# Cutting 1160 weight columns into groups of 136, 512 and 512 instead of 392, 384 and 384

## What is computed

```python
# first layer
W = L0_cond_weights[itok_B_0_15]                     # 64x64 for each of the 128 sequences
c = einsum('bct,bcd->bdt', x, W)                     # condition product
logits = c @ W_router.T                              # 8 experts
combine = normalized top-2 of softmax(logits)
h = einsum('nd,erd->ner', c, A)                      # adapters down: 8 experts x rank 16
expert_out = einsum('ner,eor->no', h * combine, B) * 2.0   # adapters up
x = x + c @ W_base.T + b_base + expert_out
# second layer
r = x @ base_weight.T + base_bias + (x @ A1[id].T) @ B1[id].T
x = x + (fp8(r / s_in) @ fp8(weight / s_w)) * (s_in * s_w) + bias
```

## Time and profile before

| | us |
|---|---|
| median of 3 runs | 1992.07 |
| lowest and highest | 1991.67, 1996.24 |
| the profiled execution | 1999.07 |
| its span, first to last instruction | 1997.3 |
| TensorE busy in it | 1970.6 |
| VectorE busy | 1424.8 |
| GpSimd busy | 494.8 |
| ScalarE busy | 399.9 |
| granted TensorE clock, mean | 0.997 |

### The profile page before, as it was taken

One profiled execution on the slowest core, in us unless ns is written; L12 is line 12 of the kernel. 1 busy time (PEld: TensorE's weight loads), 2 busy tenths in 40 slices (PEclk: granted clock), 3 DMA queues, 4 the chain that ended last, 5 costly groups with the idle time before them and its releaser, 6 DMA issues.

```text
span 1997.3 us, 37836 instructions
## 1 busy us (share of the span) xinstructions
PE 1970.6 (99%) x13056; PEld 1808.4 (91%) x13056; DVE 1424.8 (71%) x3877; ACT 399.9 (20%) x1087; POOL 494.8 (25%) x471
## 2 busy tenths in 40 slices
PE   6999999999999999999999999999999999999998
PEld 6999999999999999999988888888888888888886
DVE  7766666777777877766666677767776677667776
ACT  3111111121211112111121221222122212122121
POOL 2553444111011011011122222222222222222221
PEclk9999999999999999999999999999999999999999
DMA  6764444333433433433366556655665565655663
GB/s 210 224 208 151 125 121 133 113 105 117 127 105 105 136 108 105 123 108 97 110 178 161 155 164 166 158 160 155 171 160 163 150 170 163 157 159 160 168 159 104
DMA packets 220535, 290.16 MB, mean 145 GB/s; under 512 B 98103, under 2 KB 169785, under 8 KB 220477
## 3 DMA queue, kind: packets, MB, share of 16 engines
q1 hardware_dynamic: 220476, 289.57, 50.9%
HBM read 163.63 MB, written 109.06 MB: 137 GB/s over the span
## 4 chain that ended last, share of the span: by engine, by line
PE 95%; DVE 2%; SPq 1%; issue 1%; DMA 1%; POOL 0%; ACT 0%; DVEq 0%; ACTq 0%; POOLq 0%
PE bank_g L1027 13%; PE bank_g L1029 13%; PE bank_g L1028 13%; PE bank_g L1091 12%; PE bank_g L1090 12%; PE bank_g L1089 12%; PE bank_y L1102 11%; PE bank_y L1007 3%; PE bank_g L1135 1%; PE bank_g L1059 1%; PE bank_g L1057 1%; PE bank_g L1058 1%; DVE hwt L327 0%; DVE w0l L769 0%; PE bank_y L1111 0%
## 5 line engine op out<-in xcount | busy, mean ns | idle before, releaser
L1027 PE MATMUL bank_g<-w0h,st_h 128*128 128x384 f32 (+1 forms) x1536 | 524.7, 342 | 8.8 <-DMA wpair<-wc 3.8
L1029 PE MATMUL bank_g<-w0h,st_l 128*128 128x384 f32 (+1 forms) x1536 | 520.6, 339 | 0.0
L1028 PE MATMUL bank_g<-w0l,st_h 128*128 128x384 f32 (+1 forms) x1536 | 520.4, 339 | 0.0
L1089 PE MATMUL bank_g<-w1h,st_h 128*128 128x352 f32 x1536 | 505.2, 329 | 0.4 <-ACT val L717 0.4
L1091 PE MATMUL bank_g<-w1h,st_l 128*128 128x352 f32 x1536 | 496.0, 323 | 0.0
L1090 PE MATMUL bank_g<-w1l,st_h 128*128 128x352 f32 x1536 | 495.1, 322 | 0.0
L1027 PEld LDWEIGHTS bank_g<-w0h,st_h 128*128 128x128 f32 x1536 | 288.9, 188 | 24.1 <-issue 15.9
L775 DVE TENSOR_TENSOR st_l<-ring,st_h 128x512 fp32r<-128x512 f32 x128 | 143.1, 1118 | 227.8 <-ACT st_h L700 227.7
L1089 PEld LDWEIGHTS bank_g<-w1h,st_h 128*128 128x128 f32 x1536 | 288.6, 188 | 8.0 <-issue 0.7
L563 POOL TENSOR_TENSOR ring<-ring,b_base_sb 128x1024 f32<-128x1024 f32 x64 | 152.6, 2399 | 563.8 <-PE bank_y L1007 535.0
L1090 PEld LDWEIGHTS bank_g<-w1l,st_h 128*128 128x128 f32 x1536 | 288.3, 188 | 1.6
(11 more groups left out here) (78 smaller groups left out, 1974.4 us busy)
## 6 DMA issues: line engine op xcount, KB each, us to landing
ring<-x SPq DMA_DIRECT2D x64, 512.0 KB, 4.4
x_scratch<-ring SPq DMA_DIRECT2D x64, 512.0 KB, 2.7
x1t_scratch<-x_blocks SPq DMA_DIRECT2D x256, 128.0 KB, 2.5
ring<-x1t_scratch SPq DMA_DIRECT2D x64, 512.0 KB, 3.6
ring<-x_scratch SPq DMA_DIRECT2D x64, 512.0 KB, 5.1
out<-obuf SPq DMA_DIRECT2D x64, 512.0 KB, 2.7
b_stack<-b_split SPq DMA_DIRECT2D x384, 64.0 KB, 3.5
raw<-a_split SPq DMA_DIRECT2D x128, 128.0 KB, 4.2
```

The source lines that it names most:

```text
L1027: pe.matmul(to, st_h[:, rows], w0h[:, k, cols], start=(k == 0), stop=False)
L1028: pe.matmul(to, st_h[:, rows], w0l[:, k, cols], start=False, stop=False)
L1029: last = pe.matmul(to, st_l[:, rows], w0h[:, k, cols], start=False, stop=(k == KC - 1))
L1089: pe.matmul(to, st_h[:, rows], w1h_k[:, k, cols], start=(k == 0), stop=False)
```

## The change

The 136 adapter and router columns become group 0 alone, and the 1024 output columns are cut into two groups of 512. Nothing is left in bank 0 that goes to the output. So:

- The adapters' up products go into banks 1 and 2 only, three matmuls of 512 columns for each.
- VectorE adds two banks of 512 columns to the tile instead of three (256, 384, 384). The remainder st_l of the next tile's second half stands behind the addition of group 1, which is now the first.
- TensorE's group 0 waits for hw_done of the previous tile, where it waited for x1_done[0]; so does the first tile of the second layer.
- The weight pieces of the first tile are 8 of 136 columns and 16 of 512.

```diff
-G0_START = (0, 392, 776)
-G0_WIDTH = (392, 384, 384)
-G0_OUT = (ER + EXPERTS, 0, 0)
-G0_COL = (0, 256, 640)
+G0_START = (0, ER + EXPERTS, ER + EXPERTS + HALF)
+G0_WIDTH = (ER + EXPERTS, HALF, HALF)
+OUT_GROUPS = (1, 2)
...
                     dve.wait_ge(xb_done, n)
-                    for g in range(3):
+                    for g in OUT_GROUPS:
                         dve.wait_ge(acc_ps[g], n)
-                        width = G0_WIDTH[g] - G0_OUT[g]
-                        cols = slice(G0_COL[g], G0_COL[g] + width)
-                        dve.tensor_tensor(ring[:, r, cols], bank_g[:, g, G0_OUT[g]:G0_WIDTH[g]],
+                        cols = slice((g - 1) * HALF, g * HALF)
+                        dve.tensor_tensor(ring[:, r, cols], bank_g[:, g, :],
                                           ring[:, r, cols], ALU.add).then_inc(x1_done[g], 1)
-                        if g == 0 and more:
+                        if g == 1 and more:
                             st_lo(n, 1)
-                        elif g == 0:
+                        elif g == 1:
                             turned_lo(0, 0, 1)
...
                     for g in range(3):
-                        if prior:
+                        if prior and g == 0:
+
+                            pe.wait_ge(hw_done, t)
+                        elif prior:
 
                             pe.wait_ge(x1_done[g], t)
                         last = bank(g, n, prior, pair if g == 1 else ())
...
-                    for g in range(3):
-                        to = bank_g[:, g, G0_OUT[g]:G0_WIDTH[g]]
-                        cols = slice(G0_COL[g], G0_COL[g] + G0_WIDTH[g] - G0_OUT[g])
+                    for g in OUT_GROUPS:
+                        to = bank_g[:, g, :]
+                        cols = slice((g - 1) * HALF, g * HALF)
...
                     if lag:
                         pe.wait_ge(val_done[g], t)
+                    elif g == 0:
+                        pe.wait_ge(hw_done, TILES)
                     else:
                         pe.wait_ge(x1_done[g], TILES)
```

## The result

| | before | changed |
|---|---|---|
| median, us | 1993.55 | 2065.32 |
| lowest and highest | 1991.67, 1996.24 | 2064.6, 2066.11 |
| ratio, 95% interval | | 1.0357 [1.0341, 1.0372] |
| profiled execution, its span | 1999.07, 1997.3 | 2066.11, 2064.3 |

The changed kernel is 71.8 us slower. The forecast was 2051, with a range of 2030 to 2073.

What follows compares the result with a forecast made beforehand. TensorE's start-to-start spacings bound the kernel: wide products +2.52 and narrow -1.53 us a tile make +0.99, x 64 = +63 us, less 4.5 of waits, so 1992 + 59 = 2051.0 us, range 2030 to 2073.

Steps and rivals of the forecast that it cites:

- What bounds the kernel: First layer: TensorE, busy 300.00 of 300.00 us at full clock; a tile is the sum of start-to-start spacings, 14.14 us.
- Narrow products: Group 0, 24 products of 136 columns a tile: 115 ns each, 2.76 us against 4.29, -1.53 us a tile.
- Wide products: 54 products of 512 columns a tile: 229 ns each, 12.37 us against 9.85, +2.52 us a tile.
- The sum: Narrow and wide products together: 15.13 us a tile against 14.14, +0.99, x 64 = +63 us (+43 to +79).
- Waits that go: TensorE's waits for turned router weights in the second tile and for the bank 0 addition at two tiles: -4.5 us together.
- The first tile: The 3.8 us wait for a condition matrix stays, hanging on SyncE's queue; 2 us left either way.
- The remainder: VectorE's rounding remainder for the next tile's second half: ready at T + 2.3, wanted at T + 2.75, so no cost.
- a difference of spacings carries over: The +59 us holds against the median of 1992.07 as against the profiled execution's 1999.07, 0.35% above it.
- Columns alone: Rival: the load costs nothing beyond the stream, a narrow product takes 71 ns; about 1987 to 1989 us. Chance 0.06.
- A quicker load: Rival: a load occupies only 89 ns, which a narrow product then takes; about 2011 us. Chance 0.03.
- load and product in a row: Rival: the load is not hidden, a narrow product takes 188 or 245 ns; 2163 or 2250 us. Chance 0.11.

Runs made afterwards that it cites:

- the long row: 24 32-bit products of one width, appended behind the changed kernel's last matmul with nothing else running: 117.1 ns each at 256 columns, 230.9 at 512.
- the sweep: Changed kernel with rows of 24 matmuls appended, 512 down to 32 columns, plus shorter stationary operands and bf16: 32-bit spacings from 230.9 ns at 512 to 111.2 at 136.
- The run of bf16: Changed kernel with group 0's matmuls reading the upper halves of both 32-bit operands as bf16, same widths: 2029.53 us, ratio 1.0171 to the kernel before.
- two repairs: Group 0 in bf16, with GpSimd's bias additions waiting for the hwt copies and VectorE's remainder ahead of the first addition: 1994.68 us, ratio 0.9987 to before.

## Why the prediction was right, and where it was off

**What bounds the kernel.** Right for the layer. TensorE shows 300.00 in 300.00, clock 1.00; a tile takes as long as its spacings. That the clock is full in every slice of the page was read too strictly: a 9 stands for 90% or more, and the trace of before has three stretches of about 3.4 us each at 0.50.

**Narrow products: right, a little too dear.** The step was that the load, hidden behind 256 columns, shows behind 136. The runs with 64, 200 and 232 columns show that the width doesn't matter, and those with bf16 and with shorter stationary operands that the load does. Its size: 2.63 us a tile against 2.76 forecast (111 ns inside the group against 115, and the first at 60, since its load lies behind a wide product). That is 8 us less in all.

**Wide products: mis-sized.** 12.59 us a tile against 12.37, outside its ends of 12.29 to 12.42: +0.22, +14 us in all. The step that failed is the growth of 0.41 to 0.42 ns a column between 256 and 384. Its lower end, 123 ns for 256 columns, came from the only three such products of a tile; the long row of that width shows 117. From there to 175 at 384 it is (175.0 - 117.1) / 128 = 0.45 ns a column, and 128 columns more give 233, which is the layer's mean (12.59 / 54); the long row has 231. What was taken as a fixed part grows with the width, from 10.4 ns at 256 to 15.0 at 384 and 17.5 at 512. The first wide product behind the narrow group costs 280 ns instead of 231, another 0.05 us a tile.

**The sum.** +1.08 us a tile against +0.99, x 64 = +69 against +63. It comes out of the widths alone: both kernels stream the same columns, 30912 a tile, 12.88 us at 2.4 GHz. Before, the sweep's excess is 24 x 13.8 + 48 x 15.0 + 3 x 10.4 + 6 x 15.0 = 1172 ns; after, 54 x 17.5 + 24 x 54.6 = 2255 ns (the tiles themselves are 1.26 and 2.34 us over their columns). Of the difference of 1.08 us, 24 x (54.6 - 13.8) = 0.98 is the load that shows, and 0.10 the wide products.

**Waits that go.** Right. The second tile took 18.61 us before (35.30 to 53.91) and takes 15.22 (37.89 to 53.11), the usual time of a tile: 3.4 us less, where the added spacings alone make 1.08 more, so 4.5 us are gone, 2.69 and 1.43 of them listed waits. The forecast was 4.5. The run of bf16 added something to the 2.7 us for hwt: in the kernel before these copies take long in the second tile because GpSimd works beside them,

```profile
44.47 6.23 DVE L327 CAST hwt<-hw_parts 32x64 fp32r<-32x64 f32 x12
45.99 1.33 POOL L575 TENSOR_TENSOR w1l<-raw,w1h 128x512 fp32r<-128x512 f32 x1
47.28 2.36 POOL L563 TENSOR_TENSOR ring<-ring,b_base_sb 128x1024 f32<-128x1024 f32 x1
```

and in the changed one they take 2.39 us, since the addition is just over. It fell on the step ahead of them, which takes 0.29 us before:

```profile
45.51 2.39 POOL L562 TENSOR_TENSOR ring<-ring,b_base_sb 128x1024 f32<-128x1024 f32 x1
45.67 2.38 DVE L845 TENSOR_TENSOR hw_parts<-hw_parts 128x128 f32<-128x128 f32 x1
48.09 2.39 DVE L326 CAST hwt<-hw_parts 32x64 fp32r<-32x64 f32 x12
```

Counted from the start of the tile the router's chain begins 1.6 us sooner (at 40.83 - 37.89 = 2.94, before at 39.85 - 35.30 = 4.55), as forecast, and hwt is ready 2.8 us sooner (12.6 against 15.4). The other 1.2 us are luck: GpSimd's work happened to fall across fewer steps.

**The first tile.** 2 us were left either way; it came out +2.6 (35.30 to 37.89 at its end). The wait for a condition matrix stays, as forecast; the list puts it down to w0l, wrongly:

```profile
16.28 2.62 DVE L768 TENSOR_TENSOR w0l<-wq,w0h 128x512 fp32r<-128x512 f32 x4
26.66 0.76 PE L1025 MATMUL bank_g<-w0h,st_h 128*128 128x512 f32 x1 [4.09 <-DVE w0l L768]
```

TensorE stands ahead of the eighth step of group 1, which needs 16 pieces (8 narrow, 8 wide), and VectorE had split these by 18.90. The same step waits for the condition matrices, and the last of these lands at 26.42, where it landed at 25.12 before. It was issued sooner (22.80 against 23.28) and was under way for 3.6 us instead of 1.8, at a time when the weight pieces were still arriving; why it took longer isn't shown. So the wait ends 26.66 - 25.36 = 1.3 us later, and the 33 wide products behind it make the other 1.3.

**The remainder.** Right: ready at T + 2.25 (forecast 2.3), wanted at T + 2.71 (2.75), no wait. The statement that it would cost once the narrow products are quicker than 78 ns was borne out at 61 ns: 0.19 us a tile. That VectorE itself could come late, stopped by GpSimd, was not in the prediction and cost 22 us more there.

**The end.** By spans the change costs 67.0 us. 69 - 4.5 + 2.6 is 67.1, but the first tile's 1.1 is in both the 69 and the 2.6, and 0.8 were small delays in four later tiles of before that are gone. The second layer adds 1.2 (1004.18 us from its first product against 1002.98), where TensorE waits 4.5 us for a transfer instead of 2.3. This makes 66.4, close to the 67.0. The medians are 71.8 apart. The profiled execution of before lay 5.5 us above its median, that of the changed kernel 0.8, so "a difference of spacings carries over" was about 4.7 us short. The granted clock probably has most to do with it. In the profile of before it is 0.50 from 1022.5 to 1025.8 and from 1988.5 to 1991.8, behind waits of TensorE of 2.3 and 1.9 us. Of the other executions of before with a listed clock, the ten at 1.000 have spans of 1989.4 to 1992.0 us and the four at 0.997 have 1995.0 to 1995.3; the profiled one lists 0.997 and spans 1997.3. The changed kernel's four all list 0.997 or 0.998. That this is why the medians lie further apart than the two profiles is likely, and not shown. The forecast of 2051 missed 2065.3 by 14.3: 8.0 from the difference of the spans (67.0 against 59, most of it the 6 of the two spacings and the 2.6 of the first tile), 1.5 from the base (1992.07 became 1993.55), and 4.8 from the profiles' places above their medians.

**The rivals.** Columns alone (71 ns) decides below 74 ns a product, and came near only with bf16 loads (61 ns); even then it took two repairs to draw level. A quicker load (89 ns) and load and product in a row (188 to 245) are ruled out by 111 ns.

## What to carry to other kernels

Where each matmul has a load of its own and all are of one type, a product costs the longer of its load and its stream; here a 128-column load of 32-bit data covers 240 moving columns (111.7 ns at 240, 111.2 at 136), and a group narrower than that pays for 240. Before recutting columns, add up what each width takes over its columns, as the total of columns says nothing: of the cuts tried the even one (392, 384, 384) has the least of it, and 264, 448, 448 already loses 0.24%. When a change makes the bounding engine quicker, look at which chains of the other engines now meet; here small VectorE copies met GpSimd's long additions, and a wait put on GpSimd, busy 24% of the span, gave back 22 us. And where an instruction waits for several things, look up when each was ready: the list of waits named a remainder that had been there for over 7 us.

## What the runs showed of the hardware that I had not expected

- The spacing of 32-bit products grows by more than one cycle a column: 117.1 ns at 256, 175.0 at 384, 230.9 at 512, where columns / 2.4 gives 106.7, 160.0 and 213.3.
- What a load occupies follows the granted clock: 213 ns for 128 stationary columns at half clock, 111 at full clock.
- The granted clock fell to half in a row of 64-column products behind full loads, in which TensorE and its loads were listed as busy throughout. In the layer, with 64 and 136 columns between wide products, it stayed at 1.00.
- One small VectorE copy of 0.19 us can stand still for a whole GpSimd addition and then takes 2.39 us; a row of twelve met two additions and took 6.71 us instead of 2.39.
- Mixing bf16 and 32-bit products in threes cost about 1%: one 32-bit and two bf16 products of 384 columns take 533 ns in a row, three 32-bit ones 525.
